# A decoder block on one core: the way from self-attention into cross-attention re-scheduled

## What is computed

```python
x = x + self_attention(layernorm(x))             # 16 heads of 64, no mask
x = x + cross_attention(layernorm(x), ctx_1024)  # 16 heads of 16, one key mask for all
x = x + experts(layernorm(x))                    # 8 experts of 256 -> 512 -> 256, top 1 gate norm
```

## Time and profile before

| | |
|---|---|
| median of 3 runs | 937.71 us (935.48 to 938.57) |
| the profiled execution | 937.62 us, span 935.8 us |
| mean granted TensorE clock | 0.986 |
| PE, ACT, DVE, POOL busy | 93%, 67%, 61%, 31% of the span |
| self-attention | about 0 to 360 us |
| cross-attention, scores of group 0 to 3 | 372 to 540 us |
| experts | about 554 to 936 us |

### The profile page before, as it was taken

The page is one execution under the profiler, slowest core; times in us unless marked ns, Lnnn a source line. Parts: engine busy times, 40 slices in busy tenths (PEclk is TensorE's granted clock), DMA queues, the critical chain, the costliest instruction groups (busy, mean ns, idle before and its releaser), DMA issues.

```text
span 935.8 us, 18382 instructions
## 1 busy us (share of the span) xinstructions
PE 866.5 (93%) x6274; PEld 782.3 (84%) x6274; DVE 569.1 (61%) x1172; ACT 630.3 (67%) x1764; POOL 291.6 (31%) x342
## 2 busy tenths in 40 slices
PE   4899999999999987899999879999999999999997
PEld 3788888889888876788888769999999999999996
DVE  4798888788878875677878755454223422342223
ACT  3897788788778864798989856765454445444543
POOL 2254454445445566655746540000000000000000
PEclk9999999999999999799999999999999999999999
DMA  6300000000000005665446113320000000000000
GB/s 207 122 31 18 1 1 1 0 0 0 0 0 0 1 1 137 144 160 113 142 86 171 45 35 102 95 87 6 17 0 0 8 15 0 0 14 9 1 1 22
DMA packets 21770, 41.98 MB, mean 45 GB/s; under 512 B 3144, under 2 KB 3152, under 8 KB 21712
## 3 DMA queue, kind: packets, MB, share of 16 engines
q1 hardware_dynamic: 21120, 40.91, 16.0%
q10 hardware_dynamic: 592, 0.34, 0.2%
HBM read 30.75 MB, written 10.49 MB: 44 GB/s over the span
## 4 chain that ended last, share of the span: by engine, by line
PE 64%; DVE 15%; ACT 13%; issue 5%; DMA 2%; POOL 1%; SPq 1%; DVEq 0%; ACTq 0%; POOLq 0%
PE Y L490 23%; PE A L490 20%; PE S L490 12%; ACT probs L803 7%; PE T L585 3%; DVE PT L880 3%; DVE nm L971 2%; DVE arena L940 2%; DVE oraw L990 2%; PE O L490 2%; PE O L602 1%; DVE arena L880 1%; ACT opart L817 1%; ACT PT L811 1%; DVE st L884 1%
## 5 line engine op out<-in xcount | busy, mean ns | idle before, releaser
L880 DVE TENSOR_TENSOR PT<-probs,PT 128x512 fp32r<-128x512 f32 x128 | 89.7, 701 | 230.9 <-ACT PT L860 230.9
L490 PE MATMUL A<-XT,arena 128*128 128x512 f32 x816 | 217.9, 401 | 6.3 <-DVE arena L940 5.3
L803 ACT ACTIVATE probs<-S,nm 128x128 f32<-128x128 f32 x512 | 181.5, 371 | 45.9 <-DVE nm L971 44.2
L490 PEld LDWEIGHTS Y<-arena,PT 128*128 128x128 f32 x1536 | 200.3, 191 | 11.0 <-DVE PT L880 1.1
L490 PE MATMUL Y<-arena,PT 128*128 128x256 f32 x1536 | 204.0, 283 | 0.3
L1194 POOL TENSOR_TENSOR probs<-probs,rinv 128x512 f32<-128x512 f32 x128 | 133.4, 1042 | 208.4 <-DVE rinv L976 208.3
L490 PEld LDWEIGHTS A<-XT,arena 128*128 128x128 f32 x816 | 144.7, 190 | 36.7 <-DVE arena L940 12.3
L860 ACT ACTIVATE PT<-probs 128x512 fp32r<-128x512 f32 x128 | 80.8, 631 | 90.7 <-PE Y L490 90.2
L803 ACT ACTIVATION_READ_ACCUMULATOR probs<-S,nm 128x1 f32 x512 | 107.4, 210 | 0.0
L880 DVE TENSOR_TENSOR PT<-T,PT 128x512 fp32r<-128x512 f32 x128 | 87.5, 684 | 25.0 <-ACT PT L811 22.8
L971 DVE TENSOR_REDUCE nm<-S 128x4 f32<-128x512 f32 x128 | 87.8, 686 | 18.0 <-PE S L490 10.5
(11 more groups left out here) (106 smaller groups left out, 1300.9 us busy)
## 6 DMA issues: line engine op xcount, KB each, us to landing
wst<-in_pieces SPq DMA_DIRECT2D x52, 256.0 KB, 2.7
stage<-arena SPq DMA_DIRECT2D x32, 256.0 KB, 2.3
arena<-stage SPq DMA_DIRECT2D x48, 128.0 KB, 4.1
arena<-stage SPq DMA_DIRECT2D x24, 256.0 KB, 3.9
xs<-in_x SPq DMA_DIRECT2D x4, 512.0 KB, 5.8
craw<-in_ctxT SPq DMA_DIRECT2D x4, 512.0 KB, 4.6
out<-craw SPq DMA_DIRECT2D x4, 512.0 KB, 2.6
rowc<-in_rows ACTq DMA_DIRECT2D x1, 264.0 KB, 5.5
```

Source lines behind the costliest of these rows:

```text
L490: mm = pe.matmul(acc, lhs[a], rhs[b], start=first and i == 0, stop=last and i == 2, skip_group_check=shared)
L803: last = act.activation(probs[:, n % 4, u * P:(u + 1) * P], S[n % 2][:, u * P:(u + 1) * P], ACT.Exp, bias=nm[:, n % 4, u:u + 1], accum_out ...
L880: dve.tensor_tensor(out_, src, hi.bitcast(F32), ALU.subtract).then_inc(sem_, 1)
```

## The change

The first cross-attention group's projections all move one slot ahead (K in slot 4, Q in 5 and 6, K in 7, V in 8 and 9). SP writes Q of heads 0 to 7 to `stage` before it stacks K. This group's quads move ahead by two slots: first scores in slot 9, last in slot 24; the second group's stay in slots 27 on, so that slots 25 and 26 have no scores. POOL zeroes KS in slots 2, 3, 6 and 7, and V2 of group 1 in four pieces of 1024 columns in slots 12 to 15.

```diff
@@ -239,16 +239,16 @@
         LGV = 12
 
         XT_AT = 3
-        SCORES = (7, 11)
+        SCORES = (7, 11, 9)
         BOTH = (0, 1)
 
 
 
 
-        QK1 = ({5: (0, BOTH), 6: (1, BOTH), 7: (2, BOTH), 8: (3, BOTH)},
+        QK1 = ({4: (0, BOTH), 5: (1, BOTH), 6: (2, BOTH), 7: (3, BOTH)},
                {0: (0, (0,)), 1: (0, (1,)), 4: (1, (0,)), 5: (1, (1,)),
                 6: (2, (0,)), 7: (2, (1,)), 8: (3, (0,)), 11: (3, (1,))})
-        V1 = ({9: (0, BOTH), 10: (1, BOTH)},
+        V1 = ({8: (0, BOTH), 9: (1, BOTH)},
               {12: (0, (0,)), 13: (0, (1,)), 14: (1, (0,)), 15: (1, (1,))})
         XT1 = ((3, 4), (2, 3))
         ALL = tuple(range(TILES))
@@ -266,8 +266,9 @@
 
 
             v -= lag
+            at_scores = SCORES[2 if ph == 1 and g == 0 else ph if ph < 2 else 1]
             if name == "quad":
-                q = v - SCORES[ph]
+                q = v - at_scores
                 return [(q,)] if 0 <= q < QUADS else []
             if name in ("qk", "v"):
                 if ph == 0:
@@ -290,8 +291,8 @@
             if name in ("residual", "bias"):
                 at = QUADS - 1 if ph == 0 else RESIDUAL1[g == GROUPS - 1]
                 if name == "residual":
-                    return [()] if v - SCORES[ph] == at else []
-                part = v - SCORES[ph] - at - ((2, 0)[g == GROUPS - 1] if ph == 1 else 1)
+                    return [()] if v - at_scores == at else []
+                part = v - at_scores - at - ((2, 0)[g == GROUPS - 1] if ph == 1 else 1)
                 return [(part,)] if 0 <= part < 2 else []
             ahead = ph == 2 or ph == 1 and g > 0
             if name in ("stats", "norm"):
@@ -438,13 +439,15 @@
                 else:
                     sp.wait_ge(scores_ps, nth(SLOT, 1, g, 8 * r + 7 - QUADS))
 
-            def stack_keys(g, r):
+            def stage_keys(g, r):
 
                 sp.wait_ge(qk_lo, nth(QK_F1, 1, g, CROSS.index((r, 1))))
                 if g > 0:
                     sp.wait_ge(kq_in[r], KQ_IN * g)
                 for s in range(2):
                     sp.dma_start(stage[r, 0, s], KP[:, r, s, :].bitcast(F32)).then_inc(k_staged, 16)
+
+            def stack_keys(g, r):
                 stack_free(g, r)
                 sp.wait_ge(k_staged, STAGED * (2 * g + r + 1))
                 for i, s in enumerate((0, 1, 0)):
@@ -453,13 +456,15 @@
                                      stage[r, 0, s].rearrange("(u h d) t -> h d u t", h=2, d=DH2)[h]
                                      ).then_inc(kq_in[r], 16)
 
-            def stack_queries(g, r):
+            def stage_queries(g, r):
 
                 sp.wait_ge(qk_lo, nth(QK_F1, 1, g, CROSS.index((r, 0))))
                 if g > 0:
                     sp.wait_ge(kq_in[r], KQ_IN * g)
                 for s in range(2):
                     sp.dma_start(stage[r, 1, s], Q[:, r, s, :].bitcast(F32)).then_inc(q_staged, 16)
+
+            def stack_queries(g, r):
                 stack_free(g, r)
                 sp.wait_ge(q_staged, STAGED * (2 * g + r + 1))
                 for i, s in enumerate((0, 0, 1)):
@@ -470,8 +475,17 @@
                 if g + 1 < GROUPS:
                     sp.wait_ge(c_lo, nth(CTX, 1, g, 0))
                     context(g + 1)
-                for r, is_key in CROSS:
-                    (stack_keys if is_key else stack_queries)(g, r)
+                stage_keys(g, 0)
+                if g == 0:
+                    stage_queries(g, 0)
+                stack_keys(g, 0)
+                if g > 0:
+                    stage_queries(g, 0)
+                stack_queries(g, 0)
+                stage_queries(g, 1)
+                stack_queries(g, 1)
+                stage_keys(g, 1)
+                stack_keys(g, 1)
             experts(0)
             with sp.Fori(1, MCH // 4) as g:
                 experts(g)
@@ -788,7 +802,7 @@
                 else:
 
                     if g < 2:
-                        act.wait_ge(v_zero, 4 + 2 * g)
+                        act.wait_ge(v_zero, 4 + 4 * g)
                     else:
                         act.wait_ge(pv_ps, nth(SLOT_F2, ph, g - 2, QUADS - 1))
                     act.activation(v2(g, 0, job), v2_raw(g, job), ACT.Copy).then_inc(v_hi, 1)
@@ -1252,16 +1266,16 @@
                     rest.then_inc(c_lo, 1)
 
             def once(ph, g, n):
-                if ph == 1 and opening(g) and n in (3, 4, 8, 9):
-
-                    pool.wait_ge(oproj, nth(OPROJ, 0, GROUPS - 1, 3 if n < 8 else 5))
-                    at = (4 + 2 * (n - 3) if n < 8 else 8 + 2 * (n - 8)) * 1024
+                if ph == 1 and opening(g) and n in (2, 3, 6, 7):
+
+                    pool.wait_ge(oproj, nth(OPROJ, 0, GROUPS - 1, 3 if n < 6 else 5))
+                    at = (4 + 2 * (n - 2) if n < 6 else 8 + 2 * (n - 6)) * 1024
                     pool.memset(arena[:, at:at + 2048].bitcast(F32), 0.0).then_inc(k_zero, 1)
-                if ph == 1 and opening(g) and n in (10, 11):
+                if ph == 1 and opening(g) and n >= 12:
 
                     pool.wait_ge(pv_ps, nth(SLOT_F2, 0, GROUPS - 1, QUADS - 1))
-                    at = (N1 + N2) * 2 * PIECE + (n - 10) * 2048
-                    pool.memset(arena[:, at:at + 2048].bitcast(F32), 0.0).then_inc(v_zero, 1)
+                    at = (N1 + N2) * 2 * PIECE + (n - 12) * 1024
+                    pool.memset(arena[:, at:at + 1024].bitcast(F32), 0.0).then_inc(v_zero, 1)
                 if ph == 0 and opening(g) and n >= 12:
                     split_context(0, g, 0, n - 12)
                 if ph == 1 and opening(g) and n < 4:
```

## The result

The changed kernel takes 947.99 us (median of 4 runs, 947.12 to 949.83), the kernel before 937.33 us (4 runs). The ratio is 1.0118, 95% interval 1.0103 to 1.0132. The forecast was 936.9, at most 939.8. The profiled execution has a span of 945.3 us, 9.5 us more than before.

A forecast was written before the change was run, and what follows sets the result against it. Before 389 us the kernel was taken as bound by waits, behind it by work (PE, ACT nearly full). 937.62 + 2.0 (slot 17 late) - 2.7 (work missing later) = 936.9 us; own range 934.9 to 938.4, full range up to 939.8.

The forecast's parts named there:

- first scores: Group 0's entry, slot 9: staging and stacking DMAs end sooner, first cross-attention scores at 366.5 instead of 372.05, 5.55 us sooner.
- K's projection: Slot 4: six matmuls in 1.64 us within PE's idle time; DVE's 0.64 us wait ends, gain 0.64 us.
- the residual add ahead of the first reciprocal: DVE, slots 10 and 11: V's rest, statistics and residual add (1.27 us) put the reciprocal at 373.1, not 369.5.
- POOL's queue of slots 11 to 15: In-order POOL work from 373.3 sums to 13.8 us, so normalisation 4 starts at 387.1.
- The side estimate by the Trainium skill: DMA at 2.0 us plus bytes over 436 GB/s: Q stacked by 363, scores at 365, sum 1.5 us lower.
- Slot 17's lateness: End of the entry: slot 17 starts 2.0 us late, 1.8 from POOL's queue and 0.2 from the clock; bounds 1.0 and 3.5.
- What comes back: Slots 25 to 31: missing scores, transpositions and products with V return 2.7 us; bounds 1.3 and 4.2.
- one loop, transposition and its two copies: Thinner slots: each transposition waits for the previous PT copies, a loop of 1.75 against 1.15 us of PE work.
- The 0.64 us that I gave back there: Slots 25 and 26: 0.64 of the 1.04 us saved on PE is given back.
- My rival on the slower side: PE stays at 1.2 GHz through slots 17 and 18, 2.0 us more each: 940.9 us, chance 0.14.
- The signs of being wrong: POOL idle between 375 and 387, scores after 369, or the clock still low at 390.
- The head start: Entry: scores 5.55 us sooner, 4.6 left at normalisation 0, then lost in POOL's queue; rival keeping it: 932.7, chance 0.26.

The follow-up runs named there:

- the fastest version: Changed kernel with first scores in slot 11, V's zeroing back in slots 10 and 11, self-attention's bias adds three slots later: 934.24 us, ratio 0.9966.

## Why the prediction was wrong

**Right.** K's projection in 1.63 us in slot 4 (1.64 said); first scores at 367.60 after a wait for a DMA of 2.64 us, at the late end of what was said (365.3 to 367.6, 366.5 taken); the residual add ahead of the first reciprocal; POOL's queue of slots 11 to 15 (13.7 us; 13.8 said). The side estimate by the Trainium skill (DMA: Bandwidth & Descriptors, Anatomy of one DMA), Q's stacking there by 363 us, did not hold here; the page gives its fit for DMAs issued from GpSimd, and these are SP's.

**Slot 17's lateness, mis-sized.** I said 2.0 us with bounds of 1.0 and 3.5; it was 3.65. By the timeline, half of the 1.65 is the later first scores, passed on to the fifth normalisation (387.94 instead of 387.1). The other half is DVE's layer-norm apply (2.4 us at 386.8), which held the PT copy for which PE's next transposition waited 1.27 us. I had not costed it.

**"What comes back", the step that failed.** I said that the work missing in slots 25 to 31 returns 2.7 us, with 1.3 as the lower bound. Between slot 17 (+3.65) and step 20 in slot 31 (+2.74) only 0.9 came back, and slots 25 and 26 gave none. I priced a thin slot by one loop, transposition and its two copies, 1.75 us; slots 25 and 26 took 2.43 each. The 0.64 us that I gave back there are not worked out in the prediction: by its own loop, 1.75 against 1.15 us, it would be 1.2 in two slots, more than the 1.04 that the missing scores save. The timeline shows the slots running at the pace of several in-order queues at once: ACT's exponentials and output copy, POOL's normalisation behind DVE's reciprocal behind Q's rest. I had also moved 1.4 us of output projections into slots 23 and 24 and not asked whether those slots had room: slot 23 took its part without loss (3.10 us, 3.14 before), slot 24 became 0.8 longer (3.10, 2.30 before). The step from 15 to 16 grew by 3.0 us with a one-slot hole and by 5.55 to 5.57 with a two-slot hole, in four kernels with different entries.

**What I did not list at all, the largest part of the miss.** The output split moved too, into the slots in which POOL has inverse root and context work: 4.9 us, of which the wait is 2.98 and the clock behind it about 1.5. The text sized each queue at the entry and none at the exit, so this stood in the sum at nothing without a reason. That it is a loss of its own is shown by two kernels: 5.6 us better with the projections, residual and bias back, 2.3 with the context work ahead. My rival on the slower side, a clock that stays low through slots 17 and 18, did not happen: the granted clock is 1.00 from 390.4 to 430.5. The clock did take about 1.5 us in the last drain, where before it stayed at 1.00 in this profile; of the four other kernels with a two-slot hole one showed it there (transpositions of 1.09 us instead of 0.63) and three did not, while three kernels without a hole showed it too. From step 63 to the end the thirteen profiles take 395.9 to 397.4 us, with the kernel before the shortest, so this part is not put down to the change.

**The signs of being wrong.** None of the three came: POOL had no idle time between 375 and 387, the scores came before 369, the clock was at 1.00 at 390. All three watched the entry, and the loss that was not forecast came behind it.

**The sum by the profile.** By steps: -0.89 at step 15, +5.55, -1.92, +4.94, +0.34 to step 63, +1.48 in the drain, 9.5 us, the difference of the spans. The forecast was made by slots, and by slots it reads:

| | said | measured |
|---|---|---|
| slot 17 | +2.0 | +3.65 |
| from there to step 20 in slot 31 | -2.7 | -0.91 |
| slot 31, the wait for the output split and the clock behind it | not listed | +4.94 |
| from there to step 63 | not listed | +0.34 |
| drain and the rest | not listed | +1.48 |
| sum | -0.7 | +9.5 |

The head start, 4.45 us at step 0, was real but small at step 15, because POOL's queue ate most of it, as forecast.

**Open.** How much of slots 25 and 26 belongs to each of the three waits was not separated; that they are what the missing work turned into is read from the timeline and from the same waits in the drain of the kernel before, not shown by a run. No kernel moved the second group's quads ahead as well, which would have closed the hole at this place and kept the head start. Why the clock fell behind the wait for the output split was not tested: it fell in all three kernels in which PE waited 2.98 us there, and in none of the three in which it waited 1.65 us or less. Why bias and zeroing pay only together is argued from POOL's queue, not tested further.

## What to carry to other kernels

When one stage of a software pipeline is moved ahead, price the gap that it leaves where the next stage has not moved. Here two slots without new scores took as long as two full ones, so moving group 0 two slots ahead gained nothing behind it and still filled the entry and the exit with more work. Look in the profile of before for a place where such thin slots already run, here the last drain. List everything that moves along with the index (here output split, projection and residual), and look at each engine's queue in the slots it moves into, at the exit as well as at the entry. And put filler such as zeroing where the in-order queue idles, not between the links of a chain (3.5 us in the fastest version here, nothing measurable in two others).

## What the runs showed that was not expected

The jump at the gap was nearly the same whatever came before it: 5.55, 5.56, 5.55 and 5.57 us in four kernels whose first group ended between 3.4 us ahead and 5.4 us behind; with the output projections back in the gap it was 5.05. And for 27 scores steps (36 to 63) two kernels that differ by 8 us kept their distance to 0.1 us: such a difference is best found by subtracting start times of one repeated step, not by comparing busy shares.
